# Cross attention: the first and the last norm of a group are scaled by ScalarE instead of VectorE

## The chip, the cores and the metric

One core of one Trainium2 chip. The metric is the device time in microseconds (us) from the start to the end of one execution; the number given is the median of three runs.

## The reference, cut to what matters

x is 16 x 256 tokens of width 256. Four decoder layers come first, then the cross attention that this document is about, then a mixture of eight experts:

```python
x = _layernorm(x + _L0_attn_ref(x, ...))              # ends in layer_norm(x, final_w, final_b)
x = _layernorm(x + _L0_xattn_ref(x, ctx_768, ...))    # the stage that is changed
x = _layernorm(x + _L0_ffn_ref(x, ...))

def _layernorm(x, axis=-1, eps=1e-05):
    m = jnp.mean(x, axis=axis, keepdims=True)
    v = jnp.var(x, axis=axis, keepdims=True)
    return (x - m) / jnp.sqrt(v + eps)

def _L0_xattn_ref(x, y, Wq, bq, Wk, bk, Wv, bv, W1, b1, W2, b2):
    q, k, v = x @ Wq + bq, y @ Wk + bk, y @ Wv + bv   # 16 heads of 16, 120 context rows
    attn = softmax(q k^T / 4)
    h = relu(attn v @ W1 + b1)
    return h @ W2 + b2
```

## The kernel before, in words

The program runs three parts one after the other: `decoder`, `cross` (L1171 to L2150) and `experts`. All of it is written per engine, with semaphores set by hand; each engine's order of work is the order of the calls in its own block.

`cross` works on eight groups of 512 tokens (four tiles of 128 tokens, 256 wide). The groups run through a software pipeline: `BODIES` is range(-4, 11), and each engine has a loop over n in it. In body n the engines work on several groups at once: `has(g)` says whether group g exists. A "body" below is one turn of that loop; in steady state one takes 35 to 39 us.

Three norms of a group need a reciprocal root: the decoder's last one (norm 0, "first"), the one of x plus the decoder's output (norm 1, "sum"), and the one after the cross attention (norm 2, "last"). VectorE makes the roots of all three at once in `joint_root(n)` (L1818): norm 0 of group n, norm 1 of group n - 1 and norm 2 of group n - 5 (`LAG`), 12 tiles in columns 0 to 11 of `mean_var` and of `root`. It runs late in body n - 3. `scale_tiles` (L1847) then does (x - mean) * root for four tiles, as four tensor_scalar at L1853:

- `first_scaled(n + 2)`: x to z[0], in body n, between `last_low(n - 3, 0)` and `last_low(n - 3, 1)` (L1926). GpSimd's `add_first` (L2063: times a row, plus a row, plus x0) waits for it by `zf`, then `sum_stats` on VectorE.
- `last_scaled(n - 2)`: x in place, in body n right behind `joint_root(n + 3)`. TensorE's `turn_last(n - 2, 0)` and `(n - 2, 1)` (L1387) wait for it by `z2`.
- `sum_scaled(n + 2)`: z[0] to z[1], right behind `last_scaled`. TensorE's `turn_sum` waits for it by `z1`, and GpSimd's `add_bias` (L2068). Behind it in VectorE's order stand `maxima(n + 1, 0, 0)` (L1889) and `router_weights(n - 3)`.

TensorE's order at the end of body n is: `key_scores(n, 3, 0)`, `attend(n, 2)` (L1450), `turn_last(n - 2, 0)` and `(n - 2, 1)`, `row_scores(n + 1, 0, 1)` (L1415, which waits for `maxima(n + 1, 0, 0)`), `key_scores(n, 3, 1)` (L1437), `outputs(n - 1, 0)` (L93, from c_hT), `turn_maxima(n + 1, 0)` (L1425).

ScalarE's order in body n, as far as it matters: `query_key_high` and `query_key_full` of (n, 3) (L1615), `last_high(n - 3, 0)` and `last_full(n - 3, 0)` (L1677, L1682), `out_rows(n - 1, 2)`, `exps(n - 1, 3, 1)` (L1645), `last_high` and `last_full` of (n - 3, 1), `max_row(n, 0)` (L1639), `out_rows(n - 1, 3)`, `context_high(n + 1)` (L1603), `sum_high(n + 1, 0)` (L1609). ScalarE's body n stands about one body's end later than TensorE's body n - 1: its `last_high(n - 3, 0)` reads what TensorE turned at the end of body n - 1.

At the start of the stage ScalarE halves the weights (`c_half`, L1596) as soon as they have landed, then waits for `s_qb`; VectorE sets `s_qb` and makes the low halves (L1868) in `split_weights`, right behind `first_scaled(0)`. In the last bodies both engines also prepare the first expert's weights (`first_expert`, `first_pair_high`, `first_weights_low`). GpSimd's `context_low` (L2073) stands ahead of the next group's `add_first` in its order. SyncE issues `load_context(n + 4)` ahead of `load_x0(n + 4)`.

The last lines of the expert stage already have a norm that is scaled by ScalarE with scale and bias (L2464) beside one scaled by VectorE (L2608).

Of the kernel before, what the change touches and what calls it, by code (L numbers as in the profile page):

```python
# [62 lines left out]
def part_from_wait(engine, gate):  # L63


    engine.sem_inc(gate, 1)
# [1104 lines left out]
def cross(nc, sb, sem, psum, shared, dram):  # L1171
# [30 lines left out]
    var, square, slope = (sb(f"c_{name}", [P, NORMS * TT], F32) for name in ("var", "square", "slope"))  # L1202
    half = sb("c_half_bits", [P, NORMS * TT], mybir.dt.int32)
    root = [sb(f"c_root{i}", [P, NORMS * TT], F32) for i in range(2)]
    ROOT_STEPS = NORMS * TT + 3 + 3 * NEWTON
    xT = [[sb(f"c_xT{i}_{h}", [P, KD, GT], F16) for h in range(2)] for i in range(2)]
    xT32 = sb("c_xT32", [P, KD, GT], F32)
    h32 = sb("c_h32", [P, KF2, GT], F32)
# [49 lines left out]
    def has(n):  # L1258
        return 0 <= n < NG
# [329 lines left out]

    @block.scalar  # L1590
    def _(act):
        for s in (ctx_h, xh1, v_f, qk_f, qk_h, mrow_in, p_in, o_in, oh, h_f, h_h, xh2, xf2, powers):
            act.sem_inc(s.sem, s.credit())
        act.wait_ge(s_const, 16 * 3)
        act.wait_ge(s_w_in, 16)
# [3 lines left out]
        def context_high(n):  # L1599
            act.wait_ge(ctx_in.sem, ctx_in.after(n))  # L1600
            act.wait_ge(V_ps.sem, V_ps.after(n - 2))
            act.wait_ge(QK_ps.sem, QK_ps.after(n - 2))
            act.activation(ctx[n % 2][0][:, :, :], ctx32[:, :, :], ACT.Copy).then_inc(ctx_h.sem, 1)  # L1603

        def sum_high(n, k):
            act.wait_ge(T1_ps.sem, T1_ps.after(n, k + 1))
# [66 lines left out]
        def last_high(n, k):  # L1673
            act.wait_ge(T2_ps.sem, T2_ps.after(n, k + 1))
            if k == 0:
                act.wait_ge(R_ps.sem, R_ps.after(n - 1))
            act.activation(xT[1][0][:, k, :], work("T2", n, k)[:, :], ACT.Copy).then_inc(xh2.sem, 1)  # L1677

        def last_full(n, k):
            if k == 0:  # L1680
                act.wait_ge(xT_out.sem, xT_out.after(n - 1))
            act.activation(xT32[:, k, :], work("T2", n, k)[:, :], ACT.Copy).then_inc(xf2.sem, 1)  # L1682
# [27 lines left out]
        for n in BODIES:  # L1710
            if has(n - 2):
                hidden_full(n - 2, 1)
            if has(n - 1):
                out_rows(n - 1, 1)
                max_row(n - 1, 3)
                exps(n - 1, 2, 0)
            if has(n - 2):
                hidden_high(n - 2, 2)
                hidden_full(n - 2, 2)
            if has(n):  # L1720
                query_key_high(n, 2)
            if has(n - 1):
                exps(n - 1, 2, 1)
            if has(n - 2):
                hidden_full(n - 2, 3)
                hidden_high(n - 2, 3)
            if n == NG + 1:
                first_expert()
                first_pair_high(5)
                first_pair_high(3)  # L1730
                first_pair_high(7)
            if has(n):
                query_key_full(n, 2)
            if has(n - 1):
                exps(n - 1, 3, 0)
            if has(n):
                query_key_high(n, 3)
                query_key_full(n, 3)
            if has(n - 3):
                last_high(n - 3, 0)  # L1740
                last_full(n - 3, 0)
            if has(n - 1):
                out_rows(n - 1, 2)
                exps(n - 1, 3, 1)
            if has(n - 3):
                last_high(n - 3, 1)
                last_full(n - 3, 1)
            if n == NG + 1:
                first_pair_high(6)
                first_pair_high(4)  # L1750
                second_weights_high()
            if n == NG + 2:
                first_weights_high(7)
                first_weights_high(5)
                first_weights_high(6)
            if has(n):
                max_row(n, 0)
            if has(n - 1):
                out_rows(n - 1, 3)
            if has(n + 1):  # L1760
                context_high(n + 1)
                sum_high(n + 1, 0)
            if has(n):
                exps(n, 0, 0)
                max_row(n, 1)
            if has(n - 3):
                powers_of(n - 3)
            if n == NG + 2:
                first_weights_high(3)
            if has(n):  # L1770
                exps(n, 0, 1)
                values(n, 0)
                values(n, 1)
            if has(n + 1):
                sum_high(n + 1, 1)
            if has(n - 1):
                outputs_high(n - 1, 0)
                outputs_high(n - 1, 1)
            if n == NG:
                first_pair_high(1)  # L1780
                first_pair_high(2)
            if has(n):
                exps(n, 1, 0)
                out_rows(n, 0)
                max_row(n, 2)
                exps(n, 1, 1)
            if has(n - 1):
                hidden_full(n - 1, 0)
                hidden_high(n - 1, 0)
            if has(n + 1):  # L1790
                query_key_high(n + 1, 0)
                query_key_high(n + 1, 1)
                query_key_full(n + 1, 0)
                query_key_full(n + 1, 1)
            if has(n - 1):
                hidden_high(n - 1, 1)
# [1 line left out]

    @block.vector
    def _(dve):  # L1800
        for s in (*stats_in, rooted, zf, z1, xl1, mx_in, rd_in, on_in, ol, y_in, z2, xl2, route):
            dve.sem_inc(s.sem, s.credit())
        dve.wait_ge(s_const, 16 * 3)

# [3 lines left out]
        def x_tiles(n):  # L1808
            return lambda t: x[:, bass.ds(n * TT + t, 1), :]
# [7 lines left out]

        def joint_root(n):  # L1818

            for i, g in enumerate((n, n - 1, n - LAG)):  # L1820
                if has(g):
                    dve.wait_ge(stats_in[i].sem, stats_in[i].after(g))
                    part_from_wait(dve, shared["dve_gate"])
            for t in range(NORMS * TT):
                dve.bn_aggr(mean_var[:, t, :], stats[:, t, :]).then_inc(rooted.sem, 1)
            k = NORMS * TT
            dve.wait_ge(rooted.sem, rooted.after(n, k))
            dve.tensor_scalar(var[:, :], mean_var[:, :, 1], EPS, None, ALU.add).then_inc(rooted.sem, 1)
            dve.wait_ge(rooted.sem, rooted.after(n, k + 1))
            dve.tensor_scalar(half[:, :], var[:, :].bitcast(mybir.dt.int32), 1, None, ALU.logical_shift_right)\  # L1830
               .then_inc(rooted.sem, 1)
            dve.wait_ge(rooted.sem, rooted.after(n, k + 2))
            dve.tensor_scalar(root[0][:, :].bitcast(mybir.dt.int32), half[:, :], -1.0, float(0x5F3759DF),
                              ALU.mult, ALU.add).then_inc(rooted.sem, 1)
            for i in range(NEWTON):
                k += 3
                y, new = root[i % 2], root[(i + 1) % 2]
                dve.wait_ge(rooted.sem, rooted.after(n, k))
                dve.tensor_tensor(square[:, :], y[:, :], y[:, :], ALU.mult).then_inc(rooted.sem, 1)
                dve.wait_ge(rooted.sem, rooted.after(n, k + 1))  # L1840
                dve.scalar_tensor_tensor(slope[:, :], square[:, :], -0.5, var[:, :], ALU.mult, ALU.mult)\
                   .then_inc(rooted.sem, 1)
                dve.wait_ge(rooted.sem, rooted.after(n, k + 2))
                dve.scalar_tensor_tensor(new[:, :], slope[:, :], 1.5, y[:, :], ALU.add, ALU.mult)\
                   .then_inc(rooted.sem, 1)

        def scale_tiles(i, n, src, out, done):  # L1847

            rstd = root[NEWTON % 2]
            dve.wait_ge(rooted.sem, rooted.after(n))  # L1850
            for t in range(TT):
                at = i * TT + t
                dve.tensor_scalar(out(t), src(t), mean_var[:, at, 0:1], rstd[:, at:at + 1], ALU.subtract, ALU.mult)\  # L1853
                   .then_inc(done.sem, 1)

        def first_stats(n):
            tile_stats(0, x_tiles(n))

        def first_scaled(n):
            dve.wait_ge(z1.sem, z1.after(n - 1))  # L1860
            scale_tiles(0, n, x_tiles(n), lambda t: z[0][:, t:t + 1, :], zf)
            if n == 0:
                split_weights()

        def split_weights():
            dve.tensor_scalar(qbias[:, :], cols[:, 0:4:2], HD ** -0.5, None, ALU.mult).then_inc(s_qb, 1)
# [50 lines left out]
        def last_stats(n):  # L1917
            dve.wait_ge(y_in.sem, y_in.after(n))
            tile_stats(2, x_tiles(n))

        def last_scaled(n):
            scale_tiles(2, n + LAG, x_tiles(n), x_tiles(n), z2)

        def last_low(n, k):
            dve.wait_ge(xf2.sem, xf2.after(n, k + 1))
# [52 lines left out]
        for n in BODIES:  # L1978
# [3 lines left out]
                first_weights_sum(6)  # L1982
            if has(n - 3):
                last_low(n - 3, 0)
            if has(n + 2):
                first_scaled(n + 2)
            if has(n - 3):
                last_low(n - 3, 1)
            if n == NG + 2:
# [45 lines left out]
                maxima(n, 3, 1)  # L2035
            if 0 <= n + 3 < NG + LAG:
                joint_root(n + 3)
            if has(n - 2):
                last_scaled(n - 2)
            if has(n + 2):  # L2040
                sum_scaled(n + 2)
            if has(n + 1):
# [817 lines left out]
```

## Time and profile before

| what | value |
|---|---|
| median of three runs | 3541.78 us (3535.92 to 3551.64) |
| the profiled execution's own time | 3547.18 us |
| its span, first to last instruction | 3545.4 us |
| TensorE busy | 3327.9 us, 94% |
| VectorE busy | 2603.5 us, 73% |
| ScalarE busy | 2353.1 us, 66% |
| GpSimd busy | 1419.8 us, 40% |
| the cross stage in it | 1864 us to about 2251 us |

Times in the trace are counted from the span's start. PE is TensorE, DVE is VectorE, ACT is ScalarE, POOL is GpSimd. A busy TensorE need not be at its peak, and GpSimd's spans are rough.

### The profile page before, as it was taken

Reading aid. Unit: us, or ns where it says so; the run is one execution under the profiler, and the core shown is the slowest. Engines: PE = TensorE matmul, PEld = TensorE weight load, DVE = VectorE, ACT = ScalarE, POOL = GpSimd, SP = SyncE. Lnnn points to the kernel's source line nnn. Section 1 sums busy time; section 2 is a strip of 40 time slices with the busy share of each in tenths; the row PEclk is TensorE's granted clock in tenths of the full one; section 3 lists DMA queues with packets and bytes.
Section 4 is the critical chain, followed back from the end, with each engine's and each line's share of the span. In section 5 each row is a group of like instructions: output and inputs, shape, how many; then the busy total and the mean of one; then the engine's idle time right before and its main releaser. Section 6 shows DMA issues by size and latency. Waiting matters only on the chain. (4 is left out here: it accounts for less than half of the span.)

```text
span 3545.4 us, 90224 instructions
## 1 busy us (share of the span) xinstructions
PE 3327.9 (94%) x36704; PEld 2322.9 (66%) x36704; DVE 2603.5 (73%) x5236; ACT 2353.1 (66%) x3538; POOL 1419.8 (40%) x1308
## 2 busy tenths in 40 slices
PE   5899999999999999999994988799999999999998
PEld 3677676776767767677762655466666666666665
DVE  4666667666676766767646888898888888888867
ACT  4677777777777777777743676566666666666665
POOL 1233232332323233232324552564454444444475
PEclk8999999999999999999996899899999999999999
DMA  3100111101111011110002122100000000000001
GB/s 121 42 29 29 41 50 37 38 29 41 42 44 36 31 41 41 45 35 31 30 1 86 57 64 75 63 13 26 1 26 26 1 26 1 26 1 26 1 13 37
DMA packets 102764, 124.56 MB, mean 35 GB/s; under 512 B 17648, under 2 KB 90608, under 8 KB 100080
## 3 DMA queue, kind: packets, MB, share of 16 engines
q1 hardware_dynamic: 102352, 118.78, 10.2%
q8 instruction: 293, 4.80, 0.6%
q14 instruction: 119, 0.97, 0.1%
HBM read 50.13 MB, written 8.39 MB: 17 GB/s over the span
## 5 line engine op out<-in xcount | busy, mean ns | idle before, releaser
L2708 POOL TENSOR_TENSOR e_hT<-e_h,e_hT 128x512 f16<-128x512 f32 x512 | 614.1, 1201 | 603.6 <-ACT e_hT L2457 580.6
L1017 DVE TENSOR_REDUCE mx<-maxima_pair 128x4 f16<-128x1024 f32 (+1 forms) x384 | 470.1, 1224 | 234.7 <-PE maxima_pair L504 232.2
L2451 ACT ACTIVATE e_h<-e_h,e_b 128x512 f32<-128x512 f32 x512 | 365.3, 714 | 417.4 <-DVE e_h L2537 417.3
L93 PE MATMUL bank<-xT,w_half 128*128 128x512 f16 x2304 | 535.2, 383 | 3.9 <-DVE xT L960 3.9
L815 ACT ACTIVATE PR<-scores_pair 128x1024 f32<-128x1024 f32 x384 | 392.6, 1022 | 127.5 <-PE scores_pair L521 119.0
L1123 POOL TENSOR_TENSOR QK<-qk,QK 128x512 f16<-128x512 f32 x128 | 148.2, 1158 | 629.4 <-ACT qk L744 434.2
L2395 PE MATMUL bank<-VS,e_hT 128*128 128x256 f16 x3072 | 389.5, 273 | 5.2 <-DVE VS L2500 4.1
L2395 PE MATMUL bank<-e_w,e_hT 128*128 128x256 f16 x3072 | 388.7, 273 | 4.6 <-POOL e_hT L2708 4.3
L93 PEld LDWEIGHTS bank<-xT,w_half 128*128 128x128 f16 x2304 | 216.4, 98 | 246.1 <-issue 12.5
L2395 PEld LDWEIGHTS bank<-VS,e_hT 128*128 128x128 f16 x3072 | 300.7, 98 | 112.1 <-DVE VS L2500 4.6
L2395 PEld LDWEIGHTS bank<-e_w,e_hT 128*128 128x128 f16 x3072 | 300.6, 98 | 109.9 <-POOL e_hT L2708 6.5
L93 PE MATMUL bank<-w_half,hT 128*128 128x256 f16 x3072 | 361.1, 275 | 6.8 <-ACT oT L771 4.6
L2457 ACT ACTIVATE e_hT<-e_h 128x512 f16<-128x512 f32 x512 | 322.5, 630 | 16.2
L93 PEld LDWEIGHTS bank<-w_half,hT 128*128 128x128 f16 x3072 | 297.9, 99 | 52.7 <-ACT oT L771 5.2
L2547 DVE SCALAR_TENSOR_TENSOR x<-e_b,expert_weight,x 128x256 f32<-128x256 f32 x224 | 240.3, 1121 | 0.0
L499 PE MATMUL maxima_pair<-KS,QS 63*128 63x256 f16 (+1 forms) x2048 | 192.7, 248 | 39.4 <-DVE mx L1017 32.8
L1130 POOL TENSOR_TENSOR hT<-spare,hT 128x512 f16<-128x512 f32 x128 | 148.1, 1157 | 203.3 <-ACT hT L799 194.1
L1113 POOL TENSOR_TENSOR VS<-VS,spare 128x512 f32<-128x512 f32 x64 | 82.0, 1280 | 367.9 <-ACT VS L763 367.9
L1134 POOL TENSOR_TENSOR x<-x,spare 128x256 f32<-128x256 f32 x256 | 178.7, 736 | 86.3 <-DVE z L160 86.3
L516 PE MATMUL scores_pair<-QS,KS 64*128 64x256 f16 (+1 forms) x2048 | 188.6, 247 | 8.2 <-ACT PR L815 7.1
L808 ACT ACTIVATE spare<-bank,cols 128x512 f32<-128x512 f32 x256 | 175.0, 685 | 27.7 <-PE bank L93 24.1
L2537 DVE TENSOR_TENSOR e_h<-maxima_pair,e_common 128x512 f32<-128x512 f32 x192 | 131.1, 688 | 81.1 <-PE maxima_pair L2373 33.1
(221 smaller groups left out, 7011.1 us busy)
## 6 DMA issues: line engine op xcount, KB each, us to landing
QS<-QK SPq DMA_DIRECT2D x240, 128.0 KB, 2.1
KS<-QK SPq DMA_DIRECT2D x192, 128.0 KB, 2.1
PR<-in_expert_weights SPq DMA_DIRECT2D x16, 1024.0 KB, 4.9
stage<-in_weights SPq DMA_DIRECT2D x48, 256.0 KB, 3.5
c_x<-in_x SPq DMA_DIRECT2D x8, 512.0 KB, 4.4
xT_f<-c_xT SPq DMA_DIRECT2D x8, 512.0 KB, 3.7
stage<-xT_f SPq DMA_DIRECT2D x4, 1024.0 KB, 5.5
out<-stage SPq DMA_DIRECT2D x8, 512.0 KB, 3.5
```

What stands on the lines that cost most here:

```text
L93: last = pe.matmul(out, stat(a, k), mov(b, k), start=(k == 0 and n == 0), stop=(k == tiles - 1 and n == 2))
L499: pe.matmul(M[:, r * GT + at:r * GT + at + keys], QS[64 * r:64 * r + R_MAX, 2 * c + i, q:q + P], KS[64 * r:64 * r + R_MAX, 2 * c + i, b * ...
L516: pe.matmul(SC[:, r * GT + at:r * GT + at + queries], KS[64 * r:64 * r + R_MAX + 1, 2 * c + i, k:k + P], QS[64 * r:64 * r + R_MAX + 1, 2 * ...
L808: act.activation(h32[:, m % NH32, :], tile(kind, "H", m)[:, :], ACT.Gelu, bias=cols[:, COL["f1b"] + m:COL["f1b"] + m + 1], scale=1.0 / WS) ...
L815: act.activation(PR[c % 2][:, s, :], SC[:, :], ACT.Exp).then_inc(p_in.sem, 1)
L1017: dve.tensor_reduce(out, src, AX.X, ALU.max, negate=True).then_inc(mx_in.sem, 1)
L1134: last = pool.tensor_tensor(x[:, bass.ds(g * TT + t, 1), :], x[:, bass.ds(g * TT + t, 1), :], rows[:, row, :].unsqueeze(1), ALU.add)
L2395: last = pe.matmul(y_bank(tile), hT[r % 2][a][:, f, tile * P:(tile + 1) * P], w2[e % 2][b][:, i + f * NI, :], start=i == f == n == 0 and u ...
L2451: act.activation(h32[r % 2][:, j, :], h32[r % 2][:, j, :], ACT.Gelu, bias=b1[:, e, m:m + 1], scale=1.0 / WS)\
L2457: act.activation(hT[r % 2][0][:, f, t * GT:(t + 1) * GT], h32[r % 2][:, j, :], ACT.Copy).then_inc(h_h.sem, 1)
L2547: dve.scalar_tensor_tensor(x[:, n:n + 1, :], b2[e % 2][:, :, :], weight[:, at:at + 1], x[:, n:n + 1, :], ALU.mult, ALU.add).then_inc(bias_ ...
L2708: pool.tensor_tensor(hT[r % 2][1][:, f, part], h32[r % 2][:, j, :], hT[r % 2][0][:, f, part], ALU.subtract)\
```

## The change

`first_scaled` and `last_scaled` leave VectorE's block and become ScalarE activations (Identity, scale = root, bias = shift, both a column per tile). `joint_root` gets one more instruction that makes shift = -mean * root for all 12 columns, and at its head waits for ScalarE's readers of the columns that it will overwrite. `sum_scaled` stays on VectorE, and waits for the root alone, not for shift. `last_scaled(n - 3)` stands ahead of `last_high(n - 3, 0)` in ScalarE's body n; `first_scaled(n + 2)` behind `last_full(n - 3, 1)`, ahead of `max_row(n, 0)`. `split_weights` stays on VectorE in body -2.

```diff
-    ROOT_STEPS = NORMS * TT + 3 + 3 * NEWTON
+    shift = sb("c_shift", [P, NORMS * TT], F32)
+    ROOT_STEPS = NORMS * TT + 3 + 3 * NEWTON + 1
...
+        def norm_tile(i, n, t, out, done):
+            at = i * TT + t
+            act.activation(out, x[:, n * TT + t, :], ACT.Identity, bias=shift[:, at:at + 1],
+                           scale=root[NEWTON % 2][:, at:at + 1]).then_inc(done.sem, 1)
+
+        def first_scaled(n):
+            act.wait_ge(rooted.sem, rooted.after(n))
+            act.wait_ge(z1.sem, z1.after(n - 1))
+            for t in range(TT):
+                norm_tile(0, n, t, z[0][:, t, :], zf)
+
+        def last_scaled(n):
+            act.wait_ge(rooted.sem, rooted.after(n + LAG))
+            for t in range(TT):
+                norm_tile(2, n, t, x[:, n * TT + t, :], z2)
...
             if has(n - 3):
+                last_scaled(n - 3)
                 last_high(n - 3, 0)
...
                 last_full(n - 3, 1)
+            if has(n + 2):
+                first_scaled(n + 2)
...
         def joint_root(n):
+            if has(n - 1):
+                dve.wait_ge(zf.sem, zf.after(n - 1))
+                part_from_wait(dve, shared["dve_gate"])
+            if has(n - 1 - LAG):
+                dve.wait_ge(z2.sem, z2.after(n - 1 - LAG))
+                part_from_wait(dve, shared["dve_gate"])
...
+            dve.wait_ge(rooted.sem, rooted.after(n, k + 3))
+            dve.scalar_tensor_tensor(shift[:, :], mean_var[:, :, 0], -1.0, root[NEWTON % 2][:, :], ALU.mult, ALU.mult)\
+               .then_inc(rooted.sem, 1)
...
-            dve.wait_ge(rooted.sem, rooted.after(n))
+            dve.wait_ge(rooted.sem, rooted.after(n, ROOT_STEPS - 1))
...
-            if has(n + 2):
-                first_scaled(n + 2)
+            if n + 2 == 0:
+                split_weights()
...
-            if has(n - 2):
-                last_scaled(n - 2)
```

## Rows read from the trace of the kernel before

**Rows 1.** Windows over the cross stage, summed: us, then busy us by engine.
```profile
sum 396.00, PE 294.21 PEld 190.35 DVE 317.00 ACT 227.92 POOL 179.24; mean PE 29.42 PEld 19.04 DVE 31.70 ACT 22.79 POOL 17.92
```

**Rows 2.** Waits, 1960 to 2210 us: us in total, times, longest.
```profile
PE bank L1387 <- DVE x L1853: 14.3, 5, 3.1
...
PE maxima_pair L1415 <- DVE mx L1889: 6.9, 5, 3.8
```

**Rows 3.** Timeline, end of body 3: start, us, instruction, idle before.
```profile
2048.66 1.07 PE L1450 MATMUL bank<-PR,VS 120*32 120x256 f32 x16
2052.54 1.06 PE L1387 MATMUL bank<-ident,x 128*128 128x128 f32 x8 [2.81 <-DVE x L1853]
2054.81 0.58 PE L1415 MATMUL maxima_pair<-KS,QS 63*128 63x120 f16 x8 [1.21 <-DVE mx L1889]
...
2055.75 4.00 PE L93 MATMUL bank<-c_half,c_hT 128*128 128x256 f16 x24
...
2049.10 3.29 DVE L1853 TENSOR_SCALAR x<-x,c_mean_var,c_root 128x256 f32<-128x256 f32 x4
2052.32 1.37 DVE L1853 TENSOR_SCALAR c_z<-c_z,c_mean_var,c_root 128x256 f32<-128x256 f32 x4
...
2050.59 0.49 ACT L1615 ACTIVATE qk<-bank,c_cols 128x240 f32<-128x240 f32 x1
...
2060.10 0.59 ACT L1639 ACTIVATE mrow<-bank 4x512 f16<-4x512 f32 x1 [2.25 <-PE bank L1425]
```

**Rows 4.** Timeline, the last norm of the program, scaled by both engines.
```profile
3538.60 1.38 DVE L2608 TENSOR_SCALAR stage<-x,e_mean_var,e_root 128x256 f32<-128x256 f32 x4
3538.71 2.08 ACT L2464 ACTIVATE stage<-x,e_shift,e_root 128x256 f32<-128x256 f32 x4 [13.03 <-DVE e_shift L2600]
```

**Rows 5.** Timeline, start of the cross stage, by engine.
```profile
1875.00 3.20 ACT L1596 ACTIVATE c_half<-spare 128x3600 f16<-128x3600 f32 x1 [26.92 <-DMA spare<-in_cross_weights]
...
1878.24 5.02 DVE L1868 SCALAR_TENSOR_TENSOR c_half<-spare,c_half 128x3600 f16<-128x3600 f32 x1 [3.59 <-ACT c_half L1596]
...
1874.71 4.78 POOL L2063 TENSOR_TENSOR c_z<-c_z,c_rows 128x1024 f32<-128x1024 f32 x2 [30.51 <-DVE c_z L1853]
1879.64 5.82 POOL L2063 TENSOR_TENSOR c_z<-c_z,c_x 128x1024 f32<-128x1024 f32 x1
...
1893.43 4.77 POOL L2063 TENSOR_TENSOR c_z<-c_z,c_rows 128x1024 f32<-128x1024 f32 x2 [6.92 <-DVE c_z L1853]
...
1892.08 1.94 PE L1387 MATMUL bank<-ident,c_z 128*128 128x128 f32 x8 [30.75 <-DVE c_z L1853]
```

**Rows 6.** Timeline, body 0 on TensorE, and the sum's scaling in body 1.
```profile
1916.91 0.58 PE L1415 MATMUL maxima_pair<-KS,QS 63*128 63x120 f16 x8 [1.43 <-DVE mx L1889]
...
1972.98 3.20 DVE L1853 TENSOR_SCALAR c_z<-c_z,c_mean_var,c_root 128x256 f32<-128x256 f32 x4
```

**Rows 7.** Timeline, ends of bodies 2, 4 and 6 on TensorE.
```profile
2017.22 4.48 PE L93 MATMUL bank<-c_half,c_hT 128*128 128x256 f16 x24
...
2094.08 5.29 PE L93 MATMUL bank<-c_half,c_hT 128*128 128x256 f16 x24
...
2168.67 1.06 PE L1387 MATMUL bank<-ident,x 128*128 128x128 f32 x8 [2.81 <-DVE x L1853]
...
2170.20 2.79 PE L93 MATMUL bank<-c_half,c_hT 128*128 128x256 f16 x24
```

**Rows 8.** Timeline, the last norms of bodies 7, 8 and 9.
```profile
2196.74 1.02 ACT L1645 ACTIVATE PR<-scores_pair 120x1024 f32<-120x1024 f32 x1
...
2197.20 1.09 PE L1387 MATMUL bank<-ident,x 128*128 128x128 f32 x8
...
2222.29 1.14 ACT L1708 ACTIVATE spare<-stage 128x512 f16<-128x512 f32 x2
...
2222.17 1.94 PE L1387 MATMUL bank<-ident,x 128*128 128x128 f32 x8 [3.15 <-DVE x L1853]
...
2242.50 1.94 PE L1387 MATMUL bank<-ident,x 128*128 128x128 f32 x8 [11.81 <-DVE x L1853]
```

More of the change, by code:

```diff
@@ L1591, in _ @@
     def _(act):
-        for s in (ctx_h, xh1, v_f, qk_f, qk_h, mrow_in, p_in, o_in, oh, h_f, h_h, xh2, xf2, powers):
+        for s in (ctx_h, xh1, v_f, qk_f, qk_h, mrow_in, p_in, o_in, oh, h_f, h_h, xh2, xf2, powers, zf, z2):
             act.sem_inc(s.sem, s.credit())
@@ L1800, in _ @@
     def _(dve):
-        for s in (*stats_in, rooted, zf, z1, xl1, mx_in, rd_in, on_in, ol, y_in, z2, xl2, route):
+        for s in (*stats_in, rooted, z1, xl1, mx_in, rd_in, on_in, ol, y_in, xl2, route):
             dve.sem_inc(s.sem, s.credit())
@@ L1857, in first_stats @@
             tile_stats(0, x_tiles(n))
[L1859 to L1863, printed above, removed]
         def split_weights():
@@ L1919, in last_stats @@
             tile_stats(2, x_tiles(n))
-        def last_scaled(n):
-            scale_tiles(2, n + LAG, x_tiles(n), x_tiles(n), z2)
         def last_low(n, k):
```

## The prediction

> **What bounds the kernel now.** I read the windows over the cross stage first. They show how much of the program the change can touch: 396 us of 3545, with TensorE busy for 294 and VectorE for 317 of them [rows 1]. The views of waits say what holds TensorE in the steady part: 14.3 us in five waits for the last norm's scaling (`turn_last` behind `last_scaled`), and 6.9 us in five waits for a maximum on VectorE, of which 3.8 are one wait in body 1 [rows 2]. So about 17 us of waits stand behind instructions that leave VectorE. The timeline of one body's end then shows the order of events [rows 3], and it is the view that decides: what takes the place of VectorE's four instructions, and is it free at that moment?
>
> In body 3 TensorE is through with `attend` at 2049.7, waits 2.81 us, turns at 2052.54, and waits 1.21 us more for the maximum. VectorE has the root at 2049.1. Its four scalings take 3.29 us in place of the 1.38 that the same form takes with GpSimd idle [rows 3, 4]. But ScalarE is itself busy up to 2051.08, the end of its last query-key activation. It waits only after that. The place chosen is a place where ScalarE waits, but its wait begins 2 us after the root is there.
>
> **The price of the new instructions.** The program's last norm is scaled in just this form by ScalarE: four tiles in 2.08 us, against 1.38 on VectorE [rows 4]. I take 2.1 us for four, in both places. From the last tile to TensorE's first turn I take 0.15 us, the distance in rows 3.
>
> A rule speaks against the swap. A tile costs VectorE 0.34 us by rows 4. The Trainium skill, VectorE: DVE Perf Modes, section on the perf-mode tier table, gives fp32 tensor_scalar in SBUF two results a cycle, 1227 ns for 2048 elements; no run here shows it. By that the removed work would be worth about half (an estimate), and term 2 below 0.6 us less.
>
> **Term 1, the start of the stage: +6.6 us.** Before, `first_scaled(0)` runs as soon as VectorE has the root, and GpSimd's three additions start at 1874.71. Now it stands in ScalarE's queue behind `c_half`, which waits for the weights' transfer and ends at 1878.20 [rows 5]. So z[0] is ready at 1880.3. GpSimd's third addition took 5.82 us beside VectorE's 5.02 us of low halves, where half of its first two is 2.39: one kept the other waiting until 1883.2. Now VectorE's goes first, from 1878.24, alone and so some 1.2 us shorter, and GpSimd starts at about 1882.1 and ends 7.2 us later, at 1889.3, 3.9 after the 1885.46 of before. (If nothing kept it waiting, it would start at 1880.3 and be 2.1 late. The Trainium skill, SBUF — State Buffer, section "two separate sides", says that such a pair of instructions hold a port as an exclusive lock; the 5.82 agrees.) With the new shift instruction (0.2 us a step in the root's chain) z[1] and TensorE's first turn come 4.1 late, at 1896.2 in place of 1892.08.
>
> Then the order on ScalarE bites again. `first_scaled(1)` stands ahead of `context_high(0)` in body -1, and waits for `z1` of group 0, ready at 1896.0. So ScalarE does 2.1 us of scaling, then the context's high half, which it did right behind `c_half` before, and which takes 0.59 us; GpSimd's `context_low` (1.09 us) stands ahead of its next additions. They start at 1899.9 in place of 1893.43 [rows 5]: +6.4. VectorE's next statistics, root (+0.2) and first maximum hang on them, and TensorE's row scores on that. SyncE's queue is moved too: `load_context(1)` now waits until 1899.8 and x0's load stands behind it, landing at about 1904.7 just as the third addition wants it: nothing, at worst 1 us. Ends: +3 (the two delays half covered) to +8.
>
> **Term 2, body 0: -1.2.** VectorE's next maximum stands behind `first_scaled(2)`, four scalings of 1.37 us like those in rows 3, and TensorE waits 1.43 us for it [rows 6]. ScalarE has a wait of its own there. In bodies 1 to 5 VectorE waits for TensorE soon after, so the 1.37 are worth nothing; on ScalarE the 2.1 us fit into its wait for `turn_maxima`, 2.25 in body 3 [rows 3]. Where that cover is gone, the row's DMA goes up to 1 us later, with about 1.7 us of slack.
>
> **Term 3, shift: +0.4.** In the ends of bodies 0 and 1 the root is on the path, 0.2 us each. The two gates at its head wait for scalings done 20 us before: nothing.
>
> **Term 4, the ends of bodies 2 to 6: +0.1.** `last_scaled` can start at 2051.0, ends at 2053.1, TensorE turns at 2053.2: 0.7 later than 2052.54. The same in bodies 2, 5 and 6; 0.4 in body 4. Together +3.2. Against that, VectorE goes straight to the sum's scaling. GpSimd's instructions that stretched the last norm now stretch this one: body 1 shows it, 3.20 us with no last norm ahead of it [rows 6]. So the maximum is ready at 2049.3 + 3.2 + 1.1 = 2053.6, while TensorE turns until 2054.3: the waits for it are gone, 6.9 less body 1's 3.8, or -3.1 [rows 2]. What is late next is ScalarE.
>
> **Term 5, the end of body 7: +2.7.** TensorE did not wait here at all: it turned at 2197.20. ScalarE is busy with exponentials until 2197.76, so the turn moves to 2199.9 [rows 8].
>
> **Term 6, body 8: +1.5.** ScalarE's queue there has weight work of the experts ahead of `last_scaled(6)`, until 2223.43; so the turn comes at 2225.6, not 2222.17, 3.4 late on its own. VectorE in turn is freed of 3.9 us in its long queue of that body, which was the later of the two. Ends 0 and +3.4.
>
> **Term 7, body 9: +1.1.** The last group is a bare chain: shift 0.2, four scalings 2.1 for 1.4, and one hand-over more [rows 8].
>
> **Term 8, TensorE's clock: -1.9.** The 24 matmuls behind the turn take 2.79 us in body 6, where there was one wait of 2.81; 4.00 in body 3 and 5.29 in body 4, where a second wait came [rows 3, 7]. A matmul of 5.29 us for 24 runs at half the pace of one of 2.79: the lower of the clock's two levels, 1.2 GHz in place of 2.4. With the second wait gone but the first longer, I take half of (1.21 + 2.50). Ends -4 and +11 (below).
>
> The sum is 6.6 - 1.2 + 0.4 + 0.1 + 2.7 + 1.5 + 1.1 - 1.9 = +9.3 us, on the profiled execution's 3547.2: 3556.5. That execution was 5.4 us above the median of the runs, so against the median it is 3541.8 + 9.3 = 3551.
>
> **Rivals.** About 0.5%, or 17.7 us, is what a measurement of this kernel can tell from no change.
>
> *Slower, the clock (0.17).* The wait ahead of `turn_last` grows from 2.8 to 3.5 us in every body, and all six run what follows at 1.2 GHz. The place is the 24 matmuls and the turn: 5.29 in place of 4.48, 4.00, 5.29, again about 4.4, 2.79 and 2.79 in bodies 2 to 7 is +8.0, and 1.94 for 1.06 in four turns +3.5 [rows 3, 7, 8]; without term 8's gain this gives 9.3 + 1.9 + 11.5 = +22.7, so 3564.5. It decides from a wait of TensorE that brings the clock down by itself. For it: body 2 went slow with hardly a second wait. Against: bodies 3 and 6 turn in 1.06 after 2.81.
>
> *About nothing (0.20).* The start costs only its lower end (+3), body 8 is covered by VectorE's gain, and the clock stays up in all bodies: 3 - 1.2 + 0.4 + 0.1 + 2.7 + 0 + 1.1 - 4 = +2, so 3544.
>
> *Faster (0.03).* VectorE is the real pace-maker. The Trainium skill, Perfetto Trace Analysis, section on Scalar/DVE operations, says that if VectorE is saturated, moving work to ScalarE may make sense. As a mechanism here: both waits of rows 2 and the slow matmuls vanish in bodies 2 to 6, at most 14.3 + 3.1 + 8, less the start's 6.6: -19, so 3523. It needs ScalarE free at the root, which rows 3 deny.
>
> *The change doesn't do what it says*: "where it waits" is half true. That is in the forecast: ScalarE waits after its query-key work, and not at all in body 7 or at the start.
>
> The forecast itself, +5 to +15, has 0.60. It lies within 0.5% but for 0.01. Chances: faster 0.03; same 0.79; slower 0.18. The range goes from 3533 (the about-nothing case less the spread of the runs) to 3566 (the slow clock).
>
> **What the profile would show.** Right: TensorE's first turn of the stage near 1896 and the first row scores about 6.5 us late; ScalarE's scalings 2.1 us for four, starting at the end of the query-key work and not at the root; TensorE's waits at `turn_last` put down to ScalarE, about 3.5 us, and none for a maximum at the ends of bodies 2 to 5; c_z's scaling on VectorE at 2.5 to 3.3 us instead of 1.37; a new wait in body 7. Wrong: additions of GpSimd that start before 1880, a scaling far from 2.1 us, or 24 matmuls that all take 2.8 or all 5.3.

## The result, and the profile after

The changed kernel takes 3553.49 us in the median of 13 runs (3542.67 to 3558.76); the kernel before took 3537.44 us in 13 runs (3532.49 to 3551.64). The ratio is 1.0039, 95% interval 1.0028 to 1.005: slower by 10 to 18 us, about 14, under the 0.5% set as the bound of "same". 3551 was predicted, in a range of 3533 to 3566.

The profiled execution of the changed kernel took 3552.53 us (span 3550.7 us). First the view of waits between 1957 and 2208 us, the stretch that answers to [rows 2]:

```profile
PE bank L1388 <- ACT x L1608: 19.7, 6, 3.4
...
PE maxima_pair L1416 <- DVE mx L1912: 4.1, 1, 4.1
```

The columns are those of [rows 2]. The waits for the last norm are now for ScalarE, 3.4 us at the longest; the six include body 7's, which had none before. Of the waits for a maximum only body 1's is left. The timeline of body 3's end shows how, beside [rows 3]:

```profile
2050.40 1.07 PE L1451 MATMUL bank<-PR,VS 120*32 120x256 f32 x16
2054.91 1.06 PE L1388 MATMUL bank<-ident,x 128*128 128x128 f32 x8 [3.44 <-ACT x L1608]
2055.91 0.38 PE L1416 MATMUL maxima_pair<-KS,QS 63*128 63x120 f16 x8
...
2056.54 4.32 PE L93 MATMUL bank<-c_half,c_hT 128*128 128x256 f16 x24
...
2050.81 1.08 DVE L1873 SCALAR_TENSOR_TENSOR c_shift<-c_mean_var,c_root 128x12 f32<-128x12 f32 x1
2051.81 2.60 DVE L1882 TENSOR_SCALAR c_z<-c_z,c_mean_var,c_root 128x256 f32<-128x256 f32 x4
...
2052.33 0.49 ACT L1632 ACTIVATE qk<-bank,c_cols 128x240 f32<-128x240 f32 x1
2052.67 2.09 ACT L1608 ACTIVATE x<-x,c_shift,c_root 128x256 f32<-128x256 f32 x4
```

The four activations take 2.09 us, start behind the query-key work, and TensorE turns at once. The row scores follow with no second wait. The shift takes 1.08 us here, against 0.17 at the start of the stage: here it runs beside additions of GpSimd, and it takes over part of the stretching. ScalarE would have been free only 0.8 us after it.

The start of the stage, the answer to [rows 5], counted from ScalarE's halving of the weights (1872.89 here, 1875.00 before; the stage begins at another time in each execution, so only distances compare):

```profile
1872.89 3.20 ACT L1597 ACTIVATE c_half<-spare 128x3600 f16<-128x3600 f32 x1 [26.80 <-DMA spare<-in_cross_weights]
1876.00 2.06 ACT L1608 ACTIVATE c_z<-x,c_shift,c_root 128x256 f32<-128x256 f32 x4
1893.74 2.08 ACT L1608 ACTIVATE c_z<-x,c_shift,c_root 128x256 f32<-128x256 f32 x4 [15.67 <-DVE c_z L1882]
1895.72 0.59 ACT L1604 ACTIVATE c_ctx<-c_ctx 128x480 f16<-128x480 f32 x1
...
1876.13 3.91 DVE L1891 SCALAR_TENSOR_TENSOR c_half<-spare,c_half 128x3600 f16<-128x3600 f32 x1 [5.07 <-ACT c_half L1597]
...
1878.20 6.46 POOL L2081 TENSOR_TENSOR c_z<-c_z,c_rows 128x1024 f32<-128x1024 f32 x2 [35.99 <-ACT c_z L1608]
1884.81 2.34 POOL L2081 TENSOR_TENSOR c_z<-c_z,c_x 128x1024 f32<-128x1024 f32 x1
...
1897.43 4.77 POOL L2081 TENSOR_TENSOR c_z<-c_z,c_rows 128x1024 f32<-128x1024 f32 x2
...
1893.79 1.94 PE L1388 MATMUL bank<-ident,c_z 128*128 128x128 f32 x8 [34.45 <-DVE c_z L1882]
```

TensorE's first turn comes 20.9 us behind the halving, against 17.1; GpSimd's second set of additions 24.5 us behind it, against 18.4. The tail, with [rows 8] before:

```profile
2198.21 1.06 PE L1388 MATMUL bank<-ident,x 128*128 128x128 f32 x8 [2.58 <-ACT x L1608]
...
2199.56 4.46 PE L93 MATMUL bank<-c_half,c_hT 128*128 128x256 f16 x24
...
2229.27 1.94 PE L1388 MATMUL bank<-ident,x 128*128 128x128 f32 x8 [6.52 <-ACT x L1608]
...
2248.66 1.94 PE L1388 MATMUL bank<-ident,x 128*128 128x128 f32 x8 [10.31 <-ACT x L1608]
```

In the kernel before, body 7's 24 matmuls were these:

```profile
2198.58 2.79 PE L93 MATMUL bank<-c_half,c_hT 128*128 128x256 f16 x24
```

Body 7 has a new wait of 2.58 us, and the 24 matmuls behind it take 4.46 us in place of 2.79; the granted clock over them is 0.60, against 1.00 before. Body 8 waits 6.52 us in place of 3.15.

**Four stretches.** To compare executions, whose decoder parts differ by some us, I cut the stage at five marks, all on TensorE but the first: ScalarE's halving of the weights (c_half), the row scores that wait for the first maximum, the first 24 matmuls from c_hT (end of body 1), the same at the end of body 6, and the experts' first matmul. I call the stretches start, fill, steady (the five bodies between the third mark and the fourth) and tail. Windows of the changed kernel (width, busy us of PE, PEld, DVE, ACT and POOL, granted clock, DMA share, GB/s):

```profile
1872.90:1914.90 42.00, 8.47 (x40) 4.71 (x40) 23.26 (x78) 13.83 (x22) 22.52 (x12) 0.58 0.14 42
1914.90:1980.40 65.50, 51.19 (x481) 30.93 (x482) 45.48 (x105) 44.67 (x74) 35.16 (x26) 0.79 0.18 55
1980.40:2168.40 188.00, 166.97 (x1719) 110.37 (x1718) 153.88 (x384) 147.55 (x253) 92.24 (x72) 0.94 0.19 60
2168.40:2256.90 88.50, 58.64 (x551) 39.66 (x550) 57.21 (x213) 49.06 (x85) 24.97 (x21) 0.81 0.20 67
```

The same for the kernel before:

```profile
1875.00:1911.40 36.40, 9.07 (x40) 5.00 (x40) 25.89 (x80) 8.94 (x12) 24.08 (x12) 0.55 0.16 48
1911.40:1978.20 66.80, 51.11 (x480) 32.04 (x480) 48.31 (x111) 42.05 (x67) 35.33 (x26) 0.78 0.18 54
1978.20:2170.20 192.00, 170.76 (x1718) 112.40 (x1716) 164.22 (x406) 129.77 (x216) 92.62 (x72) 0.92 0.19 59
2170.20:2250.70 80.50, 55.06 (x551) 38.19 (x549) 67.34 (x231) 43.83 (x75) 25.76 (x21) 0.84 0.21 74
```

The steady bodies win 4.0 us. The start loses 5.6 and the tail 8.0. The table (in brackets the number of the experiment below) has the same four numbers for every kernel of the study, from one profiled execution each, and the ratio to the kernel before from all runs:

| kernel | start | fill | steady | tail | stage | ratio (95%) |
|---|---|---|---|---|---|---|
| before | 36.4 | 66.8 | 192.0 | 80.5 | 375.7 | 1 |
| before, second profile (7) | 36.9 | 65.4 | 192.3 | 81.6 | 376.2 | |
| before, third profile (8) | 36.7 | 61.2 | 190.4 | 80.5 | 368.8 | |
| changed | 42.0 | 65.5 | 188.0 | 88.5 | 384.0 | 1.0039 (1.0028 to 1.005) |
| changed, second profile (12) | 42.0 | 61.8 | 187.9 | 88.1 | 379.8 | |
| groups 0, 1 first norm on VectorE (1) | 36.0 | 62.6 | 186.1 | 88.5 | 373.2 | 1.0013 (1.0001 to 1.0025) |
| group 0 first norm on VectorE (6) | 38.9 | 65.3 | 188.4 | 88.1 | 380.7 | 1.0014 (1.0003 to 1.0025) |
| groups 5 to 7 last norm on VectorE (2) | 42.0 | 65.5 | 188.0 | 80.6 | 376.1 | 1.001 (1.0001 to 1.0019) |
| only first norms on ScalarE (3) | 42.0 | 65.5 | 191.9 | 81.5 | 380.9 | 1.0027 (1.0017 to 1.0037) |
| only last norms on ScalarE (4) | 35.5 | 61.9 | 185.9 | 88.5 | 371.8 | 1.0009 (0.9999 to 1.0019) |
| start and tail on VectorE (5) | 36.8 | 62.7 | 186.0 | 80.6 | 366.1 | 0.9993 (0.9982 to 1.0003) |
| only last norms, groups 0 to 4 (9) | 36.3 | 67.2 | 188.3 | 81.7 | 373.5 | 0.9994 (0.9983 to 1.0006) |
| the same, ahead of the keys (10) | 36.0 | 61.8 | 180.5 | 82.9 | 361.2 | 0.9986 (0.9974 to 0.9997) |
| tail: norm ahead of expert's weights (11) | 42.1 | 64.8 | 187.9 | 88.5 | 383.3 | 1.0039 (1.0026 to 1.0052) |

### The profile page after: what moved, and what is told of

It reads as the page before. It is cut to its first block and busy times, and to the rows that moved or that the text cites. A ratio compares the mean times of both kernels' runs of the same rounds, so it can differ in the third digit from the quotient of the medians.

```text
span 3550.7 us, 90251 instructions
## 1 busy us (share of the span) xinstructions
PE 3322.9 (94%) x36704; PEld 2320.7 (65%) x36704; DVE 2575.6 (73%) x5185; ACT 2382.5 (67%) x3602; POOL 1415.1 (40%) x1308
```

## The experiments

Each edit is shown against the changed kernel, in its main lines. My theory after the result: two fixed places cost the time, the start and the tail; the steady bodies gain a little. The rival: the steady bodies cost it, by longer waits at the turn and the lower clock behind them.

**1. First norms of groups 0 and 1 back on VectorE.** Here and below `first_scaled_dve` and `last_scaled_dve` are the functions of before.

```diff
             if has(n + 2):
-                first_scaled(n + 2)
+                if n + 2 >= 2:
+                    first_scaled(n + 2)
...
+            if has(n + 2) and not (n + 2 >= 2):
+                first_scaled_dve(n + 2)
             if n + 2 == 0:
                 split_weights()
```

> The changed kernel, but the first norms of groups 0 and 1 are scaled by VectorE again, where they were. My theory (two fixed places cost time: the start of the stage and its last three bodies): TensorE's first turn and the first row scores come 4 to 6 us earlier against the start of the stage than in the changed kernel, and the whole is 4 to 5 us shorter than the changed one, about 1.0026 of the kernel before. Rival (the cost is made in the steady bodies, by longer waits at the turn and the lower clock behind them): the whole stays within 1.5 us of the changed kernel, at 1.0035 to 1.004.

Measured: 3544.0 us, ratio 1.0013 (1.0001 to 1.0025). The start is 36.0 us long again. By the two ratios that is 9 us less than the changed kernel, more than the theory's 4 to 5. The trace has 6.0 us less in the start, 2.9 in the fill and 1.9 in the steady bodies, and the last two vary by as much between executions of one kernel. The rival, at most 1.5 us less, falls.

**2. Last norms of groups 5, 6 and 7 back on VectorE.**

```diff
             if has(n - 3):
-                last_scaled(n - 3)
+                if n - 3 < 5:
+                    last_scaled(n - 3)
...
+            if has(n - 2) and not (n - 2 < 5):
+                last_scaled_dve(n - 2)
```

> The changed kernel, but the last norms of groups 5, 6 and 7 (bodies 7, 8 and 9) are scaled by VectorE again. My theory: TensorE no longer waits in body 7, turns in body 8 after about 3 us of waiting in place of 6.5, and the whole is 5 to 7 us shorter than the changed kernel, about 1.0023 of the kernel before. Rival (steady bodies): within 1.5 us of the changed kernel.

Measured: 3543.61 us, ratio 1.001 (1.0001 to 1.0019). The tail is 80.6 us, 7.9 less; start, fill and steady bodies are the changed kernel's to the tenth. This is the cleanest pair of the study: the last norms of groups 5 to 7 cost 7.9 us in the trace. By the ratios it is 10 us.

**3. and 4. One half of the change each.**

```diff
-                last_scaled(n - 3)
+                if False:
+                    last_scaled(n - 3)
...
+            if has(n - 2) and not (False):
+                last_scaled_dve(n - 2)
```

That is 3, with only the first norms left on ScalarE. In 4 only the last norms are:

```diff
-                first_scaled(n + 2)
+                if False:
+                    first_scaled(n + 2)
...
+            if has(n + 2) and not (False):
+                first_scaled_dve(n + 2)
```

> Only the first norm goes to ScalarE; the last norm stays on VectorE. My theory: the cost of the start (4 to 5.5 us) less about 1 us in body 0, and nothing in the steady bodies: 1.0010 to 1.0014 of the kernel before. Rival (steady bodies): the first norm's 2.1 us on ScalarE delay the row of maxima in every body: 1.002 or more.

> Only the last norm goes to ScalarE; the first norm stays on VectorE. My theory: bodies 2 to 6 gain 0 to 4 us in sum, bodies 7 to 9 lose 6 to 8: 1.0010 to 1.0022 of the kernel before, the larger of the two parts of the change. Rival (steady bodies): nearly all of the change's 14 us, 1.003 or more, with waits of 3.4 us at the turn and the matmuls behind them at the lower clock in most bodies.

Measured: only the first norm, 3550.32 us, 1.0027 (1.0017 to 1.0037); only the last norm, 3543.1 us, 1.0009 (0.9999 to 1.0019). I had the two parts the wrong way round. The trace of the first-norm kernel has the start's 42.0 us and no gain: its steady bodies take 191.9 us, as before. So moving the first norm costs the start and buys nothing that this trace shows in the steady bodies. That of the last-norm kernel has the whole gain of the steady bodies (185.9) and the whole cost of the tail (88.5). The gain holds across the table: the steady bodies take 180.5 to 188.4 us in all ten profiles with their last norms on ScalarE, and 190.4 to 192.3 in the four with them on VectorE.

**5. Both repairs.**

> The changed kernel with both repairs: first norms of groups 0 and 1, and last norms of groups 5, 6 and 7, on VectorE as before; ScalarE keeps the first norms from group 2 on and the last norms of groups 0 to 4. If start and tail are two separate costs, the savings of the two repairs alone add up: about 9 and 10 us off the changed kernel's 1.0039, so 0.998 to 0.9995 of the kernel before, and in the trace a cross stage of about 366 us from the weights' halving to the experts' first matmul, against 384 in the changed kernel. Rival (both repairs only shifted the phase of TensorE's clock, by luck): between 1.000 and 1.002.

Measured: 3536.45 us, 0.9993 (0.9982 to 1.0003), and a stage of 366.1 us, as expected. By the ratios the two repairs save 9 and 10 us alone and 16 together, which is their sum within the spread. The rival said 1.000 to 1.002; the interval only touches its lower end, and the trace has start and tail each at the length of the kernel before. This kernel also keeps the shift instruction and its gates, so these cost nothing that can be seen in start (36.8 us) or tail (80.6).

**6. Only group 0's first norm back on VectorE.** The edit is that of 1 with `>= 1`.

> The changed kernel, but only group 0's first norm is back on VectorE; group 1's stays on ScalarE, ahead of the context's high half. It splits the start's delay, 5.6 us at the first row scores, in its two causes. My theory: the late z of group 0 is about 4 us of it and is gone; the context behind group 1's scaling is the rest, 1.5 to 2.5 us, and stays. TensorE's first turn at 16.5 us behind the halving of the weights, the first waited-for row scores at 37.5 to 38.5. Total 1.0015 to 1.003 of the kernel before. Rival (GpSimd's context work covers it all): row scores at 36, like the kernel with both groups on VectorE.

Measured: 3546.87 us, 1.0014 (1.0003 to 1.0025), at the lower edge of what was expected; the row scores at 38.9 us, just beyond it. So of the start's 5.3 us (42.0 against 36.7, the mean of three) 3.1 are the late z of group 0. The other 2.2 come with group 1's scaling on ScalarE. That they are the context's high half, which has to stand behind it, fits its 2.08 us, but no run takes the two apart.

**7. and 8. The kernel before, twice more.**

> The kernel before, unchanged, for a second profile. The first profile's time is 7 to 10 us above the median of that kernel's runs. If the difference of 14 us between the medians against 8 us in the stage comes from that one execution, this profile shows a cross stage of 368 to 372 us in place of 375.7, with fewer matmuls at the lower clock in bodies 0 and 1. If the stage is 375 to 376 us again, the missing 6 us of the change are outside of the stage.

> The kernel before, unchanged, for a third profile: the same as for the second, and how far the length of the cross stage is from one execution to the next.

Measured: 3551.17 and 3539.76 us, stages of 376.2 and 368.8 us. The second profile repeats the stage of the first, the third is one of those expected to be shorter: the stage's length varies from one execution of the same kernel to the next. Of the 11.4 us between the two, 7.4 lie in the stage, 4.2 of them in the fill. The windows over the fill in the two, first the one of 3551.17 us:

```profile
1914.50:1979.90 65.40, 51.14 (x480) 31.23 (x481) 47.34 (x111) 41.90 (x67) 35.26 (x26) 0.79 0.18 55
```

And the one of 3539.76 us:

```profile
1911.10:1972.30 61.20, 46.81 (x481) 27.85 (x482) 46.88 (x111) 41.94 (x67) 35.33 (x26) 0.86 0.19 59
```

The same instructions, at a mean granted clock of 0.79 or 0.86, take 65.4 or 61.2 us.

**9. Only the last norms of groups 0 to 4 on ScalarE.** The edit is that of 2, and all first norms on VectorE.

> Only the last norms of groups 0 to 4 are scaled by ScalarE; all first norms and the last norms of groups 5, 6 and 7 stay on VectorE. By the four stretches of the stage this joins the start and the fill of the kernel with only last norms (35.5 and 61.9 us), its steady bodies (185.9) and the tail of VectorE (80.6): 364 us against 369 to 376 of the kernel before, 0.998 to 0.9995 of it in time. If moving the first norm off VectorE had been of use in the steady bodies, it would be slower than the kernel with both norms moved from group 2 on (0.9993).

Measured: 3537.7 us, 0.9994 (0.9983 to 1.0006). That can't be told from experiment 5, where the first norms from group 2 on are on ScalarE: their place makes no difference that the runs show. The profiled stage is 373.5 us and not the 364 expected. Of the 9.5 us, 5.3 are a slow fill (67.2 us), 2.4 the steady bodies (188.3), the rest start and tail.

**10. The same, ahead of the keys' work.**

```diff
+            if has(n - 3) and n - 3 < 5:
+                last_scaled(n - 3)
             if has(n):
                 query_key_high(n, 3)
                 query_key_full(n, 3)
             if has(n - 3):
-                last_scaled(n - 3)
                 last_high(n - 3, 0)
```

> The same, and last_scaled stands ahead of the last query-key activations in ScalarE's order. If ScalarE's queue is what the turn waits for, the scaling starts 0.7 us earlier, with the shift and not at the end of the keys' work, TensorE waits 2.7 us in place of 3.4 at the turn, and each of bodies 3 to 6 is up to 0.4 us shorter (the maximum is next): 1 to 2 us in all. If the keys' work is itself on the path, the steady bodies grow by 2 us each.

Measured: 3536.64 us, 0.9986 (0.9974 to 0.9997): the only kernel of the study that is faster than the one before beyond its interval, by 1 to 9 us, and only just; among ten ratios that can be chance. From experiment 9 it can't be told by the runs. Its timeline at the end of body 3:

```profile
2035.97 2.07 ACT L1608 ACTIVATE x<-x,c_shift,c_root 128x256 f32<-128x256 f32 x4
...
2038.19 1.07 PE L1388 MATMUL bank<-ident,x 128*128 128x128 f32 x8 [2.73 <-ACT x L1608]
2039.20 0.39 PE L1416 MATMUL maxima_pair<-KS,QS 63*128 63x120 f16 x8
```

The wait at the turn is 2.73 us, as expected. The steady bodies take 180.5 us, 7.8 less than in 9, where 1 to 2 were expected; the mean granted clock in them is 0.97 in place of 0.94. This profiled execution took 3528.4 us, 8 below the median of its kernel's runs, so not all of the 7.8 is typical, and 1.2 of it comes back in the tail (82.9 against 81.7), whose first 24 matmuls take 4.39 us here.

**11. All on ScalarE, group 6's last norm ahead of the expert's weight work.**

```diff
             if n == NG + 1:
+                last_scaled(6)
                 first_expert()
...
             if has(n - 3):
-                last_scaled(n - 3)
+                if n - 3 != 6:
+                    last_scaled(n - 3)
```

> The changed kernel with group 6's last norm put ahead of the first expert's weight work in ScalarE's order, instead of behind it. All norms stay on ScalarE. If the queue is the cause of the 6.5 us wait in body 8, the wait falls by 3 us to about 3.4, and the tail from 88.5 to about 86 us: 1.003 of the kernel before. If the wait is the price of the four activations and the hand-over, it stays at 6 us or more.

Measured: 3554.04 us in four runs, 1.0039 (1.0026 to 1.0052), tail 88.5 us, where 1.003 and 86 were expected. Half of the expectation came: TensorE's wait fell from 6.52 to 3.40 us, but the next one grew from 10.31 to 13.95. The timeline of VectorE behind it:

```profile
2232.87 0.69 DVE L1948 TENSOR_TENSOR c_xT<-bank,c_xT 128x512 f16<-128x512 f32 x1 [7.14 <-ACT c_xT L1699]
2233.84 0.69 DVE L1948 TENSOR_TENSOR c_xT<-bank,c_xT 128x512 f16<-128x512 f32 x1 [0.28 <-ACT c_xT L1699]
2234.45 4.27 DVE L1988 SCALAR_TENSOR_TENSOR KS<-PR,QS 128x512 f16<-128x512 f32 x3
...
2238.64 0.68 DVE L1939 SCALAR_TENSOR_TENSOR x<-bank,x 128x512 f32<-128x512 f32 x1
```

VectorE, freed of its scaling, sat 7.14 us waiting for ScalarE, and only then came to the weights' low halves and the residuals, on which the last group hangs. Counted from the end of body 6, the first of the last group's two residuals (L1939 here) comes 67.5 us behind it, against 69.0 in the changed kernel and 61.2 in the one before. So 3.1 us less of waiting brought 1.5 us there, and even they are gone by the experts' first matmul. Two of VectorE's next instructions took them:

```profile
2239.24 2.60 DVE L2208 TENSOR_TENSOR PR<-PR 128x512 f32<-128x512 f32 x2
...
2243.09 0.92 DVE L1962 TENSOR_TENSOR c_less<-c_logit,c_top 128x32 f32<-128x32 f32 x1
```

In the changed kernel the same two took 1.84 and 0.19 us. Here both run beside additions of GpSimd (2239.69 to 2243.96), there only the first does, and in part. So the end does not hang on TensorE's wait in body 8.

**12. The changed kernel once more.**

> The changed kernel, unchanged, for a second profile. If the fill of the pipeline (bodies 0 and 1) is slow because it starts at another time relative to the rest, it takes 65.5 us again at a mean granted clock of 0.79. If it is chance from one execution to the next, as in the kernel before (66.8, 65.3, 61.2 us), any value between 61 and 67 us.

Measured: 3549.85 us; start 42.0, steady 187.9, tail 88.1, all as in the first profile; fill 61.8 at a clock of 0.86, in place of 65.5 at 0.79. So the fill's length varies from one execution to the next in this kernel too. Start and tail hardly do.

## Why the prediction was right, point by point

**The sign, the mechanism and the size of each place.** The direction is right for every term that could be measured by itself; the sizes are off by up to 1.8 us each, and the errors cancel. In the mean of the profiles the stage grew by 8.3 us: +5.3 in the start, -0.8 in the fill, -3.6 in the steady bodies, +7.4 in the tail. The terms gave +9.3.

- Price: 2.06 to 2.10 us for four activations, as read from [rows 4].
- Term 1, +6.6: +5.3 measured at the row scores, +5.6 against the first profile alone, from which the forecast was made. Against that profile the first turn came 3.8 late (4.1 forecast), the additions of group 1 6.1 (6.4). VectorE's low halves took 3.91 us with GpSimd's first addition stretched behind them, as argued: 6.46 us for two instead of 4.78. (The exclusive lock of the Trainium skill, SBUF — State Buffer, section "two separate sides", agrees: whichever starts first, here VectorE's 3.91 us, makes the other late.) One step was mis-sized: between the additions and the row scores 0.5 us came back, since one instruction of VectorE's root (c_var) took 1.51 us in place of 2.00. The forecast's sign of being wrong, "additions of GpSimd that start before 1880", is met by the letter (1878.20), but the whole stage lies 2.1 us earlier in this execution; counted from the halving the additions start 5.3 us behind it, as forecast.
- Term 2, -1.2: TensorE's wait for that maximum fell from 1.43 to 0.21 us.
- Term 3, shift at 0.2 us: wrong in size where it stands beside GpSimd, 1.08 us. It cost little: c_z's scaling behind it is stretched the less, 2.60 us where 3.20 was read from [rows 6].
- Term 4, +0.1: the waits at the turn are 3.43 us, forecast 3.5, and the waits for a maximum are gone.
- Term 8, -1.9: too small, and its reason only half true. Terms 4 and 8 together were -1.8; the steady stretch became 3.6 us shorter (188.0 against a mean of 191.6). In the first profile of each kernel the 24 matmuls of bodies 1 to 5 take 20.6 us in place of 23.4. But in bodies 2, 3 and 4, with no second wait ahead of them, they still take 4.20, 4.32 and 4.43 us (4.48, 4.00 and 5.29 before). So the clock falls there without a second wait too, and what decides which body goes slow stays open.
- Term 5, +2.7: the wait is 2.58 us. What failed is that no clock was counted behind a new wait. The 24 matmuls behind it went from 2.79 to 4.46 us, so body 7 cost 4.3. All six profiles with this wait have it: 4.41 to 4.46 us.
- Term 6, +1.5: experiment 2 against the changed kernel gives it. The second residual of the last group comes 7.0 us later behind the halving (366.85 us against 359.83 in experiment 2), of which 4.3 are body 7's: 2.7. The prediction let VectorE's freed 3.9 us pay for ScalarE's delay. They could not, since VectorE's queue waits for ScalarE's halves (8.54 us in the changed kernel) before it comes to its own long work.
- Term 7, +1.1: 0.8, what lies between that residual and the experts' first matmul (17.1 us against 16.3).

**The rivals.** The slow clock did not come as the rival had it, 24 matmuls of 5.29 us in all six bodies: they take 2.79 to 4.46, and the mean granted clock of the steady bodies rose from 0.92 to 0.94. Only in body 7 did it come true in part. Nor did the faster case. The "about nothing" case needed a start of +3 and a covered body 8.

**The base.** The terms were added to one profiled execution. It turned out to have a slow fill, and the median of the first three runs was 4.3 us above that of all 13. With the later median the same terms give 3546.7, 6.8 us short. So it is partly luck that 3551 came so close to 3553.5. The difference forecast was 9.3 us, the runs' is 10 to 18.

The stages of the profiled executions differ by 8.3 us in the mean (381.9 of two against 373.6 of three), and what lies outside the stage did not grow (3167.5 us of the span in the mean of two, 3170.7 of three). The profiled executions of the kernel before took 3546.0 us in the mean, 8.6 above the median of its 13 runs; those of the changed kernel 3551.2, 2.3 below its own. So the few profiled executions make the difference look smaller than the runs do; where the runs have the rest, some 2 to 10 us, stays open.

Open too: whether a late start makes the slow fill more frequent. With a late start (38.9 us or more) five of six profiled executions had it (64.8 us or more), without it three of eight. These are too few to tell.

## What to carry to other kernels

"Where it waits" has to be read with a time: an engine that waits ahead of an instruction may begin that wait after the operand is ready, and then the operand waits for the engine; in a pipeline's first and last bodies there may be no such wait at all. When work moves between in-order queues, price the prologue and the epilogue on their own: here they cost 13 us where five steady bodies won 4. And time freed on an engine pays for nothing if that engine's next instruction waits for the one that took the work.

## What was not expected of the hardware

In one pair of profiles a shorter wait went with more than its length. In experiment 10 the wait at the turn is 0.7 us shorter than in 9, 3.6 us over five bodies, and the steady bodies are 7.8 us shorter. The 24 matmuls behind the wait take 2.79 us in bodies 2 and 4, where they took 4.26 and 4.46 in 9 (body 3 is alike in both, body 5 went the other way, 3.59 for 2.79), and the granted clock of the stretch is 0.97 against 0.94. But the medians of the two kernels differ by 1.1 us only, so that the order of ScalarE's work causes it is not shown. In the other direction the result is firm: a new wait of 2.58 us in body 7 brought 1.6 to 1.7 us of slow matmuls in all six profiles that have it. And the same kernel, instruction for instruction, has a fill of 61.2 or of 65.4 to 66.8 us, at a granted clock of 0.86 or of 0.78 to 0.79: for the length of such a stage one profile is not good to better than 5 us.
